# Scores and exponentials of a causal attention in units of four heads over three PSUM banks, with keys, queries and values through one bank

## What is computed

```python
q = _gelu(jnp.concatenate([q_c, q_r], axis=-1)).reshape(b, s, H, HD).transpose(0, 2, 1, 3)
k = _gelu(jnp.concatenate([k_c, k_r], axis=-1)).reshape(b, s, H, HD).transpose(0, 2, 1, 3)
scale = 1.0 / math.sqrt(HD)
scores = jnp.einsum('bhqd,bhkd->bhqk', q, k) * scale
causal = jnp.triu(jnp.ones((s, s), dtype=bool), k=1)
scores = jnp.where(causal[None, None], -jnp.inf, scores)
attn = jax.nn.softmax(scores, axis=-1)
out = jnp.einsum('bhqk,bhkd->bhqd', attn, v)
out = out.transpose(0, 2, 1, 3).reshape(b, s, E)
return out @ wo + bo
```

## Time and profile before

| what | value |
|---|---|
| median of 3 runs | 2169.27 us (2168.54 to 2169.32) |
| the profiled execution's own time | 2166.51 us |
| its span, first to last instruction | 2164.8 us |
| PE, DVE, ACT, POOL busy | 1634.9, 1583.1, 1134.5, 1019.8 us |
| mean granted TensorE clock | 0.889 |
| the attention stage | 1757 us to the end |

### The profile page before, as it was taken

How to read it: one execution, slowest core, us unless ns; L and a number is a source line. 1 busy time by engine, 2 the same in 40 slices (tenths; PEclk the granted TensorE clock), 3 DMA queues, 4 the chain that set the end, 5 groups by cost and what they waited for, 6 DMA issues and landing times. The chain is left out here.

```text
span 2164.8 us, 32713 instructions
## 1 busy us (share of the span) xinstructions
PE 1634.9 (76%) x8418; PEld 1187.9 (55%) x8418; DVE 1583.1 (73%) x4335; ACT 1134.5 (52%) x1811; POOL 1019.8 (47%) x1114
## 2 busy tenths in 40 slices
PE   3186786886858758597684299898999988878876
PEld 2154454554535535364452298787888865555554
DVE  3199989999999999999998444444444457667763
ACT  1265464664636646366453154544545546666664
POOL 2766877677777867777795000000000003323332
PEclk8598888898988979789898599999999989999997
DMA  4410020110200102002000511001110000000000
GB/s 85 100 40 15 1 65 1 28 38 1 64 0 21 43 1 64 0 11 48 1 10 10 126 21 25 19 13 26 21 25 10 16 25 16 15 15 15 22 15 13
DMA packets 140675, 58.82 MB, mean 27 GB/s; under 512 B 94711, under 2 KB 135148, under 8 KB 140524
## 3 DMA queue, kind: packets, MB, share of 16 engines
q1 hardware_dynamic: 140524, 57.19, 11.8%
HBM read 36.05 MB, written 21.10 MB: 26 GB/s over the span
## 5 line engine op out<-in xcount | busy, mean ns | idle before, releaser
L594 PE MATMUL pb<-hid,wd 128*128 128x512 f32 x528 | 301.4, 656 | 192.0 <-POOL hid L406 191.1
L402 POOL TENSOR_TENSOR hid<-act_g,act_u 128x512 f32<-128x512 f32 x256 | 328.2, 1282 | 163.5 <-ACT act_c L518 148.3
L518 ACT ACTIVATE act_g<-pb 128x512 f32<-128x512 f32 (+1 forms) x264 | 158.1, 599 | 371.2 <-PE pb L545 329.6
L406 POOL TENSOR_TENSOR hid<-hid,act_c 128x512 f32<-128x512 f32 x256 | 328.7, 1284 | 21.5 <-POOL hid L402 1.8
L1762 DVE SCALAR_TENSOR_TENSOR l_acc<-l_pb,l_gtok,l_acc 128x128 f32<-128x128 f32 x512 | 144.4, 344 | 257.0 <-PE l_pb L1406 256.7
L1321 ACT ACTIVATE l_hid<-l_pb,l_cols 128x512 f32<-128x512 f32 x256 | 169.4, 688 | 183.1 <-PE l_pb L1406 182.7
L543 PE MATMUL pb<-xt_hi,wg_hi 128*128 128x512 f32 (+1 forms) x264 | 190.3, 721 | 91.3 <-ACT act_g L518 91.3
L1406 PEld LDWEIGHTS l_pb<-l_big,l_hid 128*128 128x128 f32 x2048 | 247.1, 192 | 10.6
L1406 PE MATMUL l_pb<-l_big,l_hid 128*128 128x128 f32 x2048 | 247.9, 275 | 0.0
L1406 PE MATMUL l_pb<-l_xt,l_big 128*128 128x512 f32 x768 | 219.1, 420 | 26.5 <-DVE l_rope L1694 24.9
L594 PEld LDWEIGHTS pb<-hid,wd 128*128 128x128 f32 x528 | 101.7, 206 | 246.5 <-POOL hid L406 220.1
(11 more groups left out here) (314 smaller groups left out, 3881.6 us busy)
## 6 DMA issues: line engine op xcount, KB each, us to landing
z_scratch<-zs SPq DMA_DIRECT2D x128, 81.0 KB, 3.0
zr<-z_scratch SPq DMA_DIRECT2D x8, 1296.0 KB, 8.1
x_sb<-in_L_attn_x_dram SPq DMA_DIRECT2D x32, 64.0 KB, 2.1
g_scratch<-zs SPq DMA_DIRECT2D x8, 256.0 KB, 2.8
y_scratch<-yo SPq DMA_DIRECT2D x8, 256.0 KB, 2.1
l_xs<-in_L_attn_x_dram SPq DMA_DIRECT2D x32, 64.0 KB, 1.9
l_ys<-y_scratch SPq DMA_DIRECT2D x128, 16.0 KB, 1.8
l_gs<-g_scratch SPq DMA_DIRECT2D x8, 256.0 KB, 3.0
```

The lines of the kernel that those rows point to most:

```text
L402: pool.tensor_tensor(hid1[:, :], g, u, ALU.mult).then_inc(s_h1, 1)
L406: pool.tensor_tensor(hid[:, (p + par) % 2, :], hid1[:, :], c, ALU.mult).then_inc(s_h, 1)
L518: act.activation(dst, pb[0:n, what, :], ACT.Silu if what == 0 else ACT.Copy).then_inc(s_ev, 1)
L594: last = pe.matmul(pb[:, SUM, :], wd[0:n, p, :], hid[0:n, (p + par) % 2, :], start=(p == 0), stop=(p == PAIRS), skip_group_check=True)
```

## The change

The units of `bx` now have four heads: three matmuls of 512 columns into banks 3, 4 and 5, one exponential of 1536 elements, and two causal instructions of 4 x 128 elements where there were two times two of 2 x 128. There are four such units in a pass instead of eight. For the third bank, k0, q0, k1, q1 and v all go through bank 0, each waiting for the one before to be read, and the max units move to banks 1 and 2. q1 moves from place 3 to place 6, behind the first three max units. The places of scores and values are new (`X_AT`, `V_AT`), and so are those of the output steps (`O_RAW` to `O_END`).

```diff
--- before.py
+++ after.py
@@ -996,10 +996,14 @@
-        def probs(u):
-
-            p = (pt, pt2)[u // 4][:, u % 4, :]
-            return p[:, 0:2 * N].rearrange("p (m n) -> p m n", m=2), p[:, 2 * N:3 * N].rearrange("p (m n) -> p m n", m=2)
+        def group_probs(g):
+
+            return (pt, pt2)[g // 2][:, 2 * (g % 2):2 * (g % 2 + 1), :].rearrange("p a n -> p (a n)")
+
+        def probs(g):
+
+            p = group_probs(g)
+            return p[:, 0:4 * N].rearrange("p (m n) -> p m n", m=4), p[:, 4 * N:6 * N].rearrange("p (m n) -> p m n", m=4)
 
         x2b = xs[:, 0:2, :], xs[:, 2:4, :]
@@ -1088,17 +1092,19 @@
-        UNITS = ["k0", "q0", "k1", "q1"] + ["max"] * 12 + ["v", "m"]
-        BANK = {0: 0, 1: 1, 2: 0, 3: 1, 16: 0, 17: 0}
+        UNITS = ["k0", "q0", "k1"] + ["max"] * 3 + ["q1"] + ["max"] * 9 + ["v", "m"]
         NU = len(UNITS)
         BY_ACT = [u in ("k0", "k1", "v") for u in UNITS]
         BY_DVE = [u in ("q0", "q1", "max") for u in UNITS]
         N_ACT, N_DVE = sum(BY_ACT), sum(BY_DVE)
-        MAX0, NM, XU = 4, 12, 8
+        KEYS, QUERIES = ([UNITS.index(f"{name}{half}") for half in range(2)] for name in "kq")
+        MAXIMA = [i for i, u in enumerate(UNITS) if u == "max"]
+        UNIT_BANK, MAX_BANK, SCORE_BANK = 0, 1, 3
+        NM, XU = len(MAXIMA), 4
         QUERIES_AT, KEYS_AT = {4: (0, 0), 7: (0, 2), 10: (1, 0), 13: (1, 2)}, {1: (0, 0, 4), 5: (1, 0, 2), 7: (1, 2, 2)}
-        X_AT, V_AT = (3, 4, 6, 7, 9, 10, 12, 13), (9, 11, 14, 17)
-
-        O_RAW, O_TB, O_NORM, O_OT, O_WO, O_END = 0, 1, 2, 4, 6, 7
+        X_AT, V_AT = (3, 6, 9, 12), (11, 13, 15, 17)
+
+        O_RAW, O_TB, O_NORM, O_OT, O_WO, O_END = 0, 3, 4, 6, 8, 9
 
         def max_rows(par, j):
 
...
@@ -1252,7 +1258,7 @@
                 turn(turns)
                 for k in range(2):
                     diagonal = probs(u)[k][:, :, 0:P]
-                    last = pool.affine_select(diagonal, diagonal, pattern=[[0, 2], [1, P]], base=0, channel_multiplier=-1,
+                    last = pool.affine_select(diagonal, diagonal, pattern=[[0, 4], [1, P]], base=0, channel_multiplier=-1,
                                               compare_op=ALU.is_ge, fill=0.0)
                 last.then_inc(s_cut, 1)
 
...
@@ -1338,22 +1344,22 @@
                 if u[0] == "k":
                     act.wait_ge(s_ua, b * NU + (i + 1))
                     at = 2 * N * int(u[1])
-                    act.activation(kr[par][:, at:at + 2 * N], pb[:, BANK[i], :], ACT.Identity, bias=kspare[:, :]).then_inc(s_ua_act, 1)
+                    act.activation(kr[par][:, at:at + 2 * N], pb[:, UNIT_BANK, :], ACT.Identity, bias=kspare[:, :]).then_inc(s_ua_act, 1)
...
             def masked_queries(b, par, i):
 
                 half, first = QUERIES_AT[i]
-                act.wait_ge(*read(b, 2 * half + 1))
+                act.wait_ge(*read(b, QUERIES[half]))
...
@@ -1365,8 +1371,7 @@
                 act.wait_ge(s_st, b * XU + (u + 1))
                 if u == 0:
                     act.wait_ge(s_pv, b * 4)
-                p = (pt, pt2)[u // 4][:, u % 4, :]
-                act.activation(p, pbf[:, 4 * 512:4 * 512 + 3 * N], ACT.Exp, scale=float(1.0 / np.sqrt(HD1))).then_inc(s_pt, 1)
+                act.activation(group_probs(u), pbf[:, 512 * SCORE_BANK:512 * SCORE_BANK + 6 * N], ACT.Exp, scale=float(1.0 / np.sqrt(HD1))).then_inc(s_pt, 1)
 
             def o_unit(b, i):
 
...
@@ -1502,17 +1507,17 @@
                 if u == "max":
-                    m = i - MAX0
+                    m = MAXIMA.index(i)
                     g, part = m // 3, m % 3
                     if m >= 2:
-                        pe.wait_ge(*read(b, i - 2))
+                        pe.wait_ge(*read(b, MAXIMA[m - 2]))
                     elif m == 0:
                         for n in range(2):
                             pe.wait_ge(s_mq[n], b)
                     if part == 0 and g % 2 == 0:
-                        pe.wait_ge(*read(b, g + 1))
+                        pe.wait_ge(*read(b, QUERIES[g // 2]))
                         pe.wait_ge(s_kb, b * 3 + (1, 3)[g // 2])
-                    bank = pb[:, 2 + m % 2, :]
+                    bank = pb[:, MAX_BANK + m % 2, :]
...
@@ -1522,24 +1527,20 @@
-                bank = pb[:, BANK[i], :]
+                bank = pb[:, UNIT_BANK, :]
...
-                if i == 0:
+                if u == "k0":
                     pe.wait_ge(s_ua_act, b * N_ACT)
-                elif i == 1:
-                    pe.wait_ge(s_ua_dve, b * N_DVE)
-                elif u == "v":
-                    pe.wait_ge(*read(b, 2))
                 else:
-                    pe.wait_ge(*read(b, i - 2))
+                    pe.wait_ge(*read(b, {"q0": KEYS[0], "k1": QUERIES[0], "q1": KEYS[1], "v": QUERIES[1]}[u]))
...
@@ -1559,20 +1560,21 @@
                     for n in range(2):
                         pe.wait_ge(s_mq[n], b + 1)
                 pe.wait_ge(s_pt, b * XU + u)
-                g, heads = u // 2, slice(2 * u, 2 * u + 2)
-                mm(pb[:, 4, :], kr[par][:, N * g:N * g + P], qb[par][:, heads, :].rearrange("p h n -> p (h n)"))
-                last = mm(pb[:, 5, 0:N].rearrange("p (m n) -> p m n", m=2), kr[par][:, N * g + P:N * (g + 1)], qb[par][:, heads, P:N])
+                for half in range(2):
+                    heads = slice(4 * u + 2 * half, 4 * u + 2 * (half + 1))
+                    mm(pb[:, SCORE_BANK + half, :], kr[par][:, N * u:N * u + P], qb[par][:, heads, :].rearrange("p h n -> p (h n)"))
+                last = mm(pb[:, SCORE_BANK + 2, :].rearrange("p (m n) -> p m n", m=4), kr[par][:, N * u + P:N * (u + 1)], qb[par][:, 4 * u:4 * (u + 1), P:N])
                 last.then_inc(s_st, 1)
 
             def values(b, par, g):
 
-                pe.wait_ge(s_cut, b * XU + 2 * (g + 1))
+                pe.wait_ge(s_cut, b * XU + (g + 1))
                 if g == 0:
                     pe.wait_ge(s_done, b)
                 out = pb[:, 6 + g // 2, N * (g % 2):N * (g % 2 + 1)]
...
                 for k in range(2):
                     for m in range(4):
-                        p = probs(2 * g + m // 2)[k][:, m % 2, :]
+                        p = probs(g)[k][:, m, :]
...
@@ -1802,15 +1804,15 @@
-                    dve.tensor_copy(qr[:, at:at + 2 * N], pb[:, BANK[i], :]).then_inc(s_ua_dve, 1)
+                    dve.tensor_copy(qr[:, at:at + 2 * N], pb[:, UNIT_BANK, :]).then_inc(s_ua_dve, 1)
                     return
-                m = i - MAX0
+                m = MAXIMA.index(i)
...
-                dve.wait_ge(*read(b, 2 * half))
+                dve.wait_ge(*read(b, KEYS[half]))
```

More of the change, by code:

```diff
@@ L1340, in a_unit @@
                     at = 2 * N * int(u[1])
-                    act.activation(kr[par][:, at:at + 2 * N], pb[:, BANK[i], :], ACT.Identity, bias=kspare[:, :]).then_inc(s_ua_act, 1)
+                    act.activation(kr[par][:, at:at + 2 * N], pb[:, UNIT_BANK, :], ACT.Identity, bias=kspare[:, :]).then_inc(s_ua_act, 1)
                 elif u == "v":
                     act.wait_ge(s_ua, b * NU + (i + 1))
-                    act.activation(vp[par][:, :, :, 0:HD1], pb[:, BANK[i], 0:2 * D].rearrange("p (k h c) -> p k h c", k=2, h=H1),
+                    act.activation(vp[par][:, :, :, 0:HD1], pb[:, UNIT_BANK, 0:2 * D].rearrange("p (k h c) -> p k h c", k=2, h=H1),
                                    ACT.Copy).then_inc(s_ua_act, 1)
@@ L1349, in a_unit @@
                     for j in range(2):
-                        last = act.activation(max_rows(par, j), pb[32 * j:32 * j + 2, 2:4, :].rearrange("p a (g n) -> p (a g) n", n=N), ACT.Copy)
+                        last = act.activation(max_rows(par, j), pb[32 * j:32 * j + 2, MAX_BANK:MAX_BANK + 2, :].rearrange("p a (g n) -> p (a g) n", n=N), ACT.Copy)
                     last.then_inc(s_mq[0], 1)
@@ L1530, in a_unit @@
                             src = mhl[:, k, h:h + 4, :].rearrange("p j c -> p (j c)").bitcast(F32)
-                            at = 2 * 512 + N * (h // 4) + P * k
+                            at = 512 * MAX_BANK + N * (h // 4) + P * k
                             last = pe.transpose(pbf[:, at:at + P], src, ident[:, :])
@@ L1795, in a_unit @@
                     for j in range(2, 4):
-                        last = dve.tensor_copy(max_rows(par, j), pb[32 * j:32 * j + 2, 2:4, :].rearrange("p a (g n) -> p (a g) n", n=N))
+                        last = dve.tensor_copy(max_rows(par, j), pb[32 * j:32 * j + 2, MAX_BANK:MAX_BANK + 2, :].rearrange("p a (g n) -> p (a g) n", n=N))
                     last.then_inc(s_mq[1], 1)
@@ L1812, in a_unit @@
                     dst, heads = mrow[:, 1, 4 * g + 2 * (part - 1):4 * g + 2 * part], 2
-                dve.tensor_reduce(dst, pb[:, 2 + m % 2, :].rearrange("p (j n) -> p j n", j=heads), AX.X, ALU.max).then_inc(s_ua_dve, 1)
+                dve.tensor_reduce(dst, pb[:, MAX_BANK + m % 2, :].rearrange("p (j n) -> p j n", j=heads), AX.X, ALU.max).then_inc(s_ua_dve, 1)
                 if m == NM - 1:
```

## The result

The changed kernel takes **2216.06 us** (median of 4 runs, 2212.63 to 2216.55) against 2168.9 us (2167.75 to 2169.32) for the kernel before, run beside it: a ratio of 1.0216, interval [1.02, 1.0233]. The profiled execution took 2216.13 us, 49.6 more than that of before; the forecast was +38.8, a median of 2208 us within 2181 to 2223.

A forecast was written before the change was run, and what follows sets the result against it. The prediction took the circle of waits between DVE and PE as the bound. Order 13.4, clock falls 25.4 and stage ends 0 summed to +38.8 on a profiled 2166.51, so 2205.3, median 2208 us; range 2181 to 2223.

The forecast's parts named there:

- The bound and the two stands: DVE and PE waiting on each other set the pass; DVE idles 1.3 us before the first maximum, 0.96 before the fifth.
- The order's term: Attention passes at full clock: the new order of waits adds 0.96 us a pass, +13.4 us; +7 to +18 possible.
- the middle and the stream: Pass from first to fifth maximum, claimed +1.47 us; then from the fifth maximum to the next "m", claimed -0.07.
- The stand for `oT`: At `wo`, PE waits for ACT's oT copy behind the masking of queries; DVE stands 0.96 us a pass for it.
- All 14 passes fall: PE's hole ahead of q0 grows from 2.79 to 3.66 us, so the clock falls in every full pass: +25.4 us.
- The price of a fall: Each clock fall in a full pass was taken to cost 2.1 us, the middle between 1.33 and 2.8.
- The ends of the stage: First and second pass and tail of the attention stage: taken as 0 us, within 3.
- Causal zeros: Instructions half as many, twice as wide: 0.8 or 1.6 us a group, hidden; uncovered, under 0.5 us a pass.
- Same clock: Rival: waits as worked out, but only three or four clock falls at 2.1; +15.7 us, median 2185; chance 0.18.
- A second fall: Rival: the wait for oT makes another 2.0 us PE hole, later maxima run at half clock; median 2243; chance 0.08.
- Faster: Rival: head scores and transposes run while DVE masks keys, oT is copied in time; -16 us, median 2153; chance 0.06.
- no change: Rival: oT's wait is covered, pass +0.0, and the clock falls stay as they are; 2172 us; chance 0.06.

The follow-up runs named there:

- the last run: The changed kernel with the output steps at their old places, plus 10 extra matmuls behind k0 and 3 ahead of k1: 2176.29 us, ratio 1.0047.

## Why the forecast was right, and where its terms were off

**The bound and the two stands: right.** The circle of DVE and PE sets the pass, and the order lengthens it at its two named places. At full clock (the pass from 1952.69 of the run with all stands filled) the pieces measure: "m" to first maximum 8.48 (forecast 8.45), first to fifth maximum 6.66 (6.50), fifth maximum to the next "m", at 1977.66, 9.83 (9.65).

**The order's term was undersized.** Forecast +0.96 a pass, +13.4; measured, with all 14 passes of either kernel at full clock, 348.9 - 330.2 = 18.6, or 1.33 a pass, just over the upper end of its bounds. The missing 0.37 lies almost all in the middle and the stream, 0.16 and 0.18: reading errors of the size that I had allowed for, but all of one sign. (The scores of group 1 stand in the prediction's text as 0.84 and in its sum as 0.87.) The stand for `oT` was right: 0.97 measured, and the early copy gives back 1.07.

**All 14 passes fall: right, its reason only in part.** That the hole of 3.74 alone is enough is shown: with the later stands filled, 14 of 14 passes still fall. But the step "2.79 is borne eleven times in 14, so what is shorter does no harm", by which the stands at `wo` and ahead of k1 got no fall, failed. A lone stand of 1.87 to 1.89 brought the clock down in seven passes of 14, two of 0.75 and 0.94 in four of 14, and the same 2.79 in three, nine or 13 of 14, as the rest of the pass was the old one, the old one with one bank, or the new. The trace of the kernel before had held a sign of it. In the turn ahead of its 14 passes (1775.37 to 1799.06, clock 0.86) the longest stand is 2.34, and the clock fell 1.5 us behind it, just as the next stand began:

```profile
1778.61 0.39 PE L1406 MATMUL l_pb<-l_kh,l_rep 128*128 128x256 f32 x1 [2.34 <-ACT l_wqk L1341]
...
1782.26 1.01 PE L1406 MATMUL l_pb<-l_big,l_xt 128*128 128x512 f32 x2 [2.08 <-ACT l_big L1369]
```

```profile
1778.00:1780.00 2.00, 1.39 (x10) 1.00 0.00 0
1780.00:1782.00 2.00, 0.18 (x2) 0.52 0.00 0
```

Length alone does not decide. The falls come every second pass in the run with only `wo` open and every fifth in the kernel before, so the moment of the stand may count; but in the last run they are three, five and four passes apart. That is argued, not shown, and stays open.

**The price of a fall was undersized.** Forecast 2.1, the middle of 1.33 and 2.8. The 14 passes take 384.0 us, and the same at full clock 348.9 (the run with all stands filled): 35.2 for the falls of 14 passes, 2.5 a pass, 2.4 in the steady ones. Most of it is one piece: from the cast of q0 to the first maximum 5.88 us instead of 3.56, since what lies between (k1, scores, transposes, the first max unit) is a chain on PE that runs at half clock from end to end. The term's upper end was the nearer one. A fall that comes at `wo` costs less, 26.24 - 24.97 = 1.27, but there the pass has a mean clock of 0.93, at the head 0.87, so it is also a shorter one. With equal mean clocks (0.86 and 0.87) it was 1.33 in the kernel before and is 2.4 now.

**Sum.** Order 18.6 (forecast 13.4); falls 35.2, less 4.3 for the three of before, 30.9 (forecast 25.4): 49.5, and 49.6 is the difference of the two executions. Both terms were some 5 too small, so that the time fell into the range is owed to the width of the range. The ends of the stage gave the 0 that I took, but by luck in part: the first "m" comes 3.7 later (1779.11 against 1775.37), 0.9 of it from ahead of the stage (its first projection starts at 1757.49 against 1756.61), and the stretch behind the last one is 3.7 shorter (31.2 to 27.5).

**Causal zeros: hidden, as forecast.** POOL takes 1.22 us for two of 512 elements, between the bounds 0.8 and 1.6, and PE never waits for them.

```profile
1955.75 1.22 POOL L1261 TENSOR_SCALAR_AFFINE_SELECT l_big<-l_big 128x512 f32<-128x512 f32 x2
```

**The rivals.** "Same clock" fell: 14 falls, not three. Its source was the Trainium skill, "TensorE: Matmul & The Clock Gate", section "Part 4: PE-mode transpose", that a transpose does not count as busy in the same way. Whether it does is still open: behind the hole to q0 without any transposes inside (3.74) the clock fell each time, and behind the one of 2.79 closed by transposes in three of 14 passes in the kernel before but in 13 of 14 with the old output places, so these rows speak for neither. "A second fall" was there in the first three of the 14 passes, behind the stand of 1.88 at `wo`, and in none of the other eleven; with the old output places it came in ten of 14. What I had held against it, that 2.0 is less than what eleven passes bore, is the step that failed. "Faster" and "no change" needed the stand at `wo` to be covered; it was 1.88.

The same page of the Trainium skill, section "A second HAM failure mode: psum-queue depth-cycling", describes, for bf16 matmuls of 512 columns, a clock that goes up and down under short idles of TensorE between groups of matmuls. The runs agree: stands of 1.88, 0.48 and 0.21 in one pass are enough for it.

## What to carry to other kernels

Split a slow-down in a loop bound by latency into the pass at full clock and the falls of TensorE's clock: filling PE's stands with matmuls that nothing reads gives the first by itself, and here was also the cheapest gain (0.23% for the kernel before). Fill every stand of the pass, not the longest alone: the changed kernel kept nine falls with the first one cut to 1.13 us, and seven with `wo` alone open. When an output step is moved behind longer work on another engine, look for the short copy that PE waits for: this one of 0.37 us cost 1.07 us a pass, and one place earlier in ACT's program that was gone. Before a bank is given up, price the chain of hand-overs that it makes: here 0.86 a pass in the old order.

## What the runs showed of the hardware that I had not expected

- A stand of PE of 1.88 us, the only one over 0.5 us in its pass, was followed by a fall to 1.2 GHz in seven passes of 14, and stands of 0.75 and 0.94 us, the longest of their pass, in four of 14.
- With stands of 0.83, 0.68 and 0.54 us a pass (the kernel before, filled) the clock fell in none of 14.
- A fall with a mean clock of 0.86 or 0.87 in the pass costs 1.33 us in the kernel before and 2.4 in the changed one, where a longer chain on PE stands behind it.
